# A graph and LSTM kernel whose row gathers each wait for an earlier gather to land

## The chip, the cores and the metric

The kernel runs on one core of one Trainium2 chip. The metric is the device time of one execution in microseconds (us), from the first to the last instruction and what the device adds around them. The engines are named as in the profile: PE (TensorE, matrix products), PEld (its weight loads), DVE (VectorE), ACT (ScalarE), POOL (GpSimd) and SP (SyncE, which only issues transfers here). A name with a q behind it (PEldq, SPq, POOLq) is that engine's sequencer, which handles waits, branches and register loads.

## The reference

Three stages are computed. The second one, the graph stage, is the one that the change touches.

```
n = layernorm(x)                                  # 6250 nodes x 512
agg = segment_sum(n[src], dst, 6250)              # 100000 edges, sorted by dst
h = relu((n + agg) @ W1 + b1)
x = x + relu(h @ W2 + b2)
# then, over 50 groups of 125 rows, as an LSTM:
f, i, o = sigmoid([z_t, h] @ W + b); g = tanh(...)  # z = layernorm(x)
c = f * c + i * g;  h = o * tanh(c)
x = x + hs
```

All of it is float32. `src` and `dst` are only known when the kernel runs, so rows of the normalized table are fetched by index.

## The kernel before

**Three parts.** `table_part` (0 to 189 us of the span) writes the normalized table, already multiplied by W1, to DRAM. `graph_part` (189 to about 1616 us) goes through 50 blocks of 125 destination nodes. `lstm_part` takes the rest. The change is in `graph_part` alone.

**One block of the graph stage.** The edges of a block are cut into 16 columns of 128 edges (`COLUMNS = 16`); the few edges beyond 2048 (7 blocks have some) are handled by a branch that is taken at run time. Each column goes through four engines:

- POOL issues an indirect DMA, the gather (line 811), which fetches 128 rows of 2 KB from `ln_table` into one of 16 buffers `rows` (in the profile `kept`, because they lie in the same memory as the LSTM's tensor of that name). It waits on `s_low` for DVE to be done with the buffer's last content, 16 gathers ago. When it has landed, it adds 16 to `s_rows[j]`, one semaphore for each of the 16 buffers.
- ACT (line 851) rounds the rows to a short format, `high` (in the profile `shared`). It waits for the landing on `s_rows[j]`, and on `s_visit` for PE to be done with what the same one of the 8 `high` buffers held.
- DVE (line 1014) subtracts to get `low_part` and adds 1 to `s_low`. It also makes the one-hot matrices (line 1006).
- PE (line 904) multiplies one-hot by high and by low into `agg`, and adds 1 to `s_visit`. One such pair is called a visit.

**The layers of the block before** run between the columns. DVE adds `agg` to the block's own table rows (`hin`, line 1053) when PE has raised `s_agg`, which it does with the first product behind the block's last visit; for block 0 a `drain` does it (line 989). PE turns `hin` (line 918), ACT applies relu (line 863), PE multiplies by W2 (lines 950, 954), DVE forms x1 and its statistics, ACT makes `z` and rounds the turned `z` (`zT_high`, line 886), and PE makes the four banks of gate inputs `gps` (line 924), which DVE adds to biases (line 1035) and SP stores.

**What sets the order.** Each engine's instructions stand in a fixed order in its function `one`, and every exchange is a semaphore. POOL's part is written out for all 50 blocks, 16 gathers one behind the other, with the branch for extra edges behind each block. The other engines run a loop over the blocks. `range_of` (line 727) loads three numbers of a block (edges before, extra columns, first edge) from `ranges` into registers with one TENSOR_LOAD; SP calls it for each load of edge lists, and ACT, PE and DVE call it once for each block. POOL calls it inside its branch only, and reads the number of extra columns of five blocks at once (line 738).

Of the kernel before, what the change touches and what calls it, by code (L numbers as in the profile page):

```python
# [42 lines left out]
LANDED = 16  # L43
# [554 lines left out]
def graph_part(nc, x, edges, table, x1_rows, gate_rows, Wx, W2s, b1c, b2r, bgr, s_w, WEIGHTS_LOADED,  # L598
# [24 lines left out]
    with ExitStack() as ctx:  # L623
        LATER = K // 2
        LAST = LATER + 1
        MOST = -(-E // P)
# [41 lines left out]
        s_rows = [sem(ctx, f"s_rows{j}") for j in range(LANDED)]  # L668
# [57 lines left out]

        def range_of(e, b):
            _, (before, extra, begin) = nc.values_load_multi_w_load_instructions(
                ranges[0:1, bass.ds(b, 1), 0:3].rearrange("o b n -> o (b n)"), engines=[e.engine],
                min_val=0, max_val=E, skip_runtime_bounds_check_because="the first part bounds it")  # L730
            extra = nc.s_assert_within(extra, 0, MOST, skip_runtime_bounds_check_because="the first part bounds it")
            begin = nc.s_assert_within(begin, 0, E, skip_runtime_bounds_check_because="the first part bounds it")
            return before, extra, begin

        CHECKED = 5

        def extras_of(e, b):
# [5 lines left out]
        def beyond_of(e, visit):  # L743
            def beyond(b):
                before, extra, begin = range_of(e, b)
                with e.If(extra > 0):
                    with e.Fori(0, extra) as g:
                        visit(before + g, g, begin)
            return beyond
# [4 lines left out]
        def _(e):  # L754
# [4 lines left out]
            def load_ends(b):  # L759
                begin = range_of(e, b)[2]  # L760
                if not isinstance(b, int) or b > 0:
                    hold(e, s_passed, s_ends, b * 16)
                e.dma_start(ends[:, bass.ds(b, 1), :, :].rearrange("p o n two -> p (o n two)"),
                            edges[bass.ds(begin, P * COLUMNS)].rearrange("(p n) two -> p (n two)", p=P)
                            ).then_inc(s_ends, 16)
# [40 lines left out]
        def _(e):  # L806
            def gather(n, b, j):
                if j == 0:
                    hold(e, s_passed, s_ends, b * 16 + 16)
                e.wait_ge(s_low, n + 1)  # L810
                e.indirect_dma_start(  # L811
                    out=rows[j % RING][:, :], out_offset=None, in_=table[:, :],
                    in_offset=bass.IndirectOffsetOnAxis(ap=ends[:, b, j, 0:1], axis=0),
                ).then_inc(s_rows[j % LANDED], 16)
# [16 lines left out]
            for b in range(BLOCKS):  # L831
                if b % CHECKED == 0:
                    extras = extras_of(e, b)
                for j in range(COLUMNS):
                    gather(b * COLUMNS + j, b, j)
                with e.If(extras[b % CHECKED] > 0):
                    before, extra, begin = range_of(e, b)
                    with e.Fori(0, extra) as g:
                        gather_beyond(before + g, g, begin)
# [7 lines left out]
        def _(e):  # L847
# [4 lines left out]

            def high_beyond(n, g, begin):
# [44 lines left out]
        def _(e):  # L898
# [8 lines left out]

            def visit_beyond(n, g, begin):
                e.wait_ge(s_hot_x, n + 2)
# [87 lines left out]
        def _(e):  # L997
# [18 lines left out]

            def beyond_columns(n, g, begin):
                e.wait_ge(s_visit_x, n + 1)
# [980 lines left out]
```

## Time and profile before

| what | value |
|---|---|
| time, median of 3 runs | 2981.14 us (2975.06 to 2987.83) |
| span of the profiled execution | 2970.5 us |
| PE busy over the span | 2593.4 us (87%) |
| DVE, ACT, POOL busy | 2147.9, 1564.9, 1009.0 us |
| gathers, line 811 | 800, mean 1046 ns of POOL each |
| queue of POOL's transfers (q0) | 240.39 MB |
| queue of SP's transfers (q1) | 370.08 MB |

The page gives no time for the profiled execution other than its span. A row that groups instructions is read so: line, engine, operation, output<-inputs, count, busy time, mean, and then the time for which the engine had been idle just before, with what ended that idle time. "remote" stands where the trace found no instruction that ended the wait. Busy PE time is partly modelled: the ends of matrix products are not measured.

### The profile page before, as it was taken

Reading aid. Unit: us, or ns where it says so; the run is one execution under the profiler, and the core shown is the slowest. Engines: PE = TensorE matmul, PEld = TensorE weight load, DVE = VectorE, ACT = ScalarE, POOL = GpSimd, SP = SyncE. Lnnn points to the kernel's source line nnn. Section 1 sums busy time; section 2 is a strip of 40 time slices with the busy share of each in tenths; the row PEclk is TensorE's granted clock in tenths of the full one; section 3 lists DMA queues with packets and bytes.
Section 4 is the critical chain, followed back from the end, with each engine's and each line's share of the span. In section 5 each row is a group of like instructions: output and inputs, shape, how many; then the busy total and the mean of one; then the engine's idle time right before and its main releaser. Section 6 shows DMA issues by size and latency. Waiting matters only on the chain. (4 is left out here: it accounts for less than half of the span.)

```text
span 2970.5 us, 47617 instructions
## 1 busy us (share of the span) xinstructions
PE 2593.4 (87%) x10746; PEld 1893.3 (64%) x10747; DVE 2147.9 (72%) x5785; ACT 1564.9 (53%) x3986; POOL 1009.0 (34%) x1018
## 2 busy tenths in 40 slices
PE   7966988878889888898888799899999799989997
PEld 6844766657667666676666566666666455655554
DVE  7745766767777677676676588777777777768886
ACT  5643444444444444444443566566656576757775
POOL 0236656655666566565653100000000000013333
PEclk9978999989999998899989899999999899999998
DMA  9657776767777777677766776577777666569995
GB/s 239 182 146 210 209 218 202 221 198 208 220 220 220 214 214 214 197 217 211 216 205 199 194 190 169 173 241 239 237 241 236 169 171 171 166 158 251 252 253 142
DMA packets 194202, 611.09 MB, mean 206 GB/s; under 512 B 41822, under 2 KB 47966, under 8 KB 164394
## 3 DMA queue, kind: packets, MB, share of 16 engines
q1 hardware_dynamic: 120432, 370.08, 42.0%
q0 software_dynamic: 73712, 240.39, 29.6%
q8 instruction: 18, 0.29, 0.0%
q14 instruction: 40, 0.33, 0.0%
HBM read 468.71 MB, written 141.62 MB: 205 GB/s over the span
## 5 line engine op out<-in xcount | busy, mean ns | idle before, releaser
L811 POOL DMA_INDIRECT kept<-ln_table,kept x800 | 836.7, 1046 | 554.7 <-DVE shared L1014 307.6
L1502 PE MATMUL acc<-shared,state 128*125 128x512 f32 x2244 | 775.0, 416 | 62.8 <-DVE state L1798 47.3
L851 ACT ACTIVATE shared<-kept 128x512 fp32r<-128x512 f32 x800 | 449.3, 626 | 403.7 <-remote 223.3
L1502 PEld LDWEIGHTS acc<-shared,state 128*125 128x125 f32 x2244 | 401.2, 187 | 198.9 <-ACT acc L1433 66.1
L904 PE MATMUL agg<-shared,onehot 128*125 128x512 f32 x1200 | 433.4, 463 | 33.0 <-DVE shared L1014 17.3
L1343 POOL TENSOR_TENSOR out<-h,lx 125x512 f32<-125x512 f32 x50 | 64.5, 1289 | 1122.6 <-DVE h L1823 1122.6
L904 PEld LDWEIGHTS agg<-shared,onehot 128*125 128x125 f32 x1200 | 254.1, 220 | 104.5 <-issue 37.1
L1502 PE MATMUL acc<-W_low,state 128*125 128x512 f32 x800 | 316.5, 396 | 0.0
L1502 PE MATMUL acc<-last_high,state 128*125 128x512 f32 x748 | 298.6, 399 | 0.0
L1014 DVE TENSOR_TENSOR shared<-kept,shared 128x512 fp32r<-128x512 f32 x400 | 267.1, 687 | 14.8 <-ACT shared L851 7.6
L924 PE MATMUL gps<-Wx_high,zT_high 128*125 128x512 f32 x800 | 226.0, 405 | 39.6 <-ACT zT_high L886 33.7
L1014 DVE TENSOR_TENSOR low_part<-kept,shared 128x512 fp32r<-128x512 f32 x400 | 256.2, 689 | 2.9 <-issue 2.5
L924 PE MATMUL gps<-Wx_low,zT_high 128*125 128x512 f32 x800 | 223.9, 402 | 0.0
L924 PE MATMUL gps<-Wx_high,zT_low 128*125 128x512 f32 x800 | 210.6, 395 | 0.0
L924 PEld LDWEIGHTS gps<-Wx_high,zT_high 128*125 128x125 f32 x800 | 152.1, 191 | 83.9 <-issue 44.7
L1425 ACT ACTIVATE tc<-c 125x128 f32<-125x128 f32 x600 | 153.7, 303 | 91.3 <-DVE c L1815 91.1
L1399 ACT ACTIVATE gate<-acc 125x512 f32<-125x512 f32 x200 | 119.6, 598 | 155.5 <-PE acc L1502 154.8
L1805 DVE TENSOR_TENSOR c<-gate,c 125x256 f32<-125x256 f32 x300 | 126.2, 421 | 84.5 <-ACT gate L1399 82.7
L924 PEld LDWEIGHTS gps<-Wx_low,zT_high 128*125 128x125 f32 x800 | 152.9, 191 | 38.7
L904 PE MATMUL agg<-low_part,onehot 128*125 128x512 f32 x400 | 165.5, 414 | 9.9 <-issue 9.7
L924 PEld LDWEIGHTS gps<-Wx_high,zT_low 128*125 128x125 f32 x800 | 148.5, 186 | 37.6
L1502 PEld LDWEIGHTS acc<-W_low,state 128*125 128x125 f32 x800 | 150.3, 188 | 30.8
(235 smaller groups left out, 4295.4 us busy)
## 6 DMA issues: line engine op xcount, KB each, us to landing
xg<-total_rows SPq DMA_DIRECT2D x100, 896.0 KB
xg<-gate_rows SPq DMA_DIRECT2D x88, 896.0 KB
gate_rows<-gout SPq DMA_DIRECT2D x200, 224.0 KB
total_rows<-total SPq DMA_DIRECT2D x50, 896.0 KB
kept<-ln_table,kept POOLq DMA_INDIRECT x800
lx<-x_rows POOLq DMA_DIRECT2D x50, 250.0 KB, 7.3
out_dram<-out POOLq DMA_DIRECT2D x50, 250.0 KB, 2.9
held<-in_x_dram SPq DMA_DIRECT2D x25, 448.0 KB
```

The lines of the kernel that those rows point to most:

```text
L811: e.indirect_dma_start(out=rows[j % RING][:, :], out_offset=None, in_=table[:, :], in_offset=bass.IndirectOffsetOnAxis(ap=ends[:, b, j, 0: ...
L851: e.activation(high[j % PARTS][:, :], rows[j % RING][:, :], ACT.Copy).then_inc(s_high, 1)
L904: m = e.matmul(agg[0:L, :], onehot[:, j % HOT_RING, :], part[j % PARTS][:, :], start=(j == 0 and part is high), stop=(part is low_part), s ...
L924: products.append(e.matmul(gps[n][0:L, :], state[:, k, :], weights[:, k, n // 2, n % 2].rearrange("p s c -> p (s c)"), start=(begins and k ...
L1014: e.tensor_tensor(low_part[j % PARTS][:, :], rows[j % RING][:, :], high[j % PARTS][:, :].bitcast(F32), ALU.subtract).then_inc(s_low, 1)
L1343: e.tensor_tensor(out[par][0:L, :], h[par][0:L].rearrange("c k u -> c (k u)"), x1[par][0:L, :], ALU.add).then_inc(s_out, 1)
L1399: e.activation(gates[0:L, half, 0].rearrange("c s u -> c (s u)"), sums, ACT.Sigmoid).then_inc(s_fi[half], 1)
L1425: e.activation(cell_turned[0:L, k], cell[0:L, k], ACT.Tanh).then_inc(s_tc[k], 1)
L1502: m = e.matmul(acc[n][0:L, :], stationary[:, k, :], weights[k][:, n * PAIR:(n + 1) * PAIR], start=begins, stop=(k == K - 1), skip_group_ch ...
L1805: e.tensor_tensor(half_of(cell, half), gates[0:L, half, 0, 0].rearrange("c (k u) -> c k u", k=KH), half_of(cell, half), ALU.mult).then_inc ...
```

## The change

Before gather n is issued, POOL also waits until gather n-3 has landed (`FLYING = 3`), on the same `s_rows` semaphores on which ACT waits. Beside it, `range_of` is taken apart in three functions of one number each, so that each place loads only what it uses; in the branch for extra columns that makes two loads where there was one.

```diff
-        def range_of(e, b):
-            _, (before, extra, begin) = nc.values_load_multi_w_load_instructions(
-                ranges[0:1, bass.ds(b, 1), 0:3]...
+        def extra_of(e, b):
+            _, (extra,) = nc.values_load_multi_w_load_instructions(
+                ranges[0:1, bass.ds(b, 1), 1:2]...
+        def begin_of(e, b):
+            _, (begin,) = ... ranges[0:1, bass.ds(b, 1), 2:3]...
+        def before_of(e, b):
+            _, (before,) = ... ranges[0:1, bass.ds(b, 1), 0:1]...
+                min_val=0, max_val=BLOCKS * MOST)
 
         CHECKED = 5
+        FLYING = 3
...
             def beyond(b):
-                before, extra, begin = range_of(e, b)
+                extra = extra_of(e, b)
                 with e.If(extra > 0):
+                    before = before_of(e, b)
                     with e.Fori(0, extra) as g:
-                        visit(before + g, g, begin)
+                        visit(before + g)
...
             def load_ends(b):
-                begin = range_of(e, b)[2]
+                begin = begin_of(e, b)
...
                 e.wait_ge(s_low, n + 1)
+                if n >= FLYING:
+                    e.wait_ge(s_rows[(n - FLYING) % LANDED], ((n - FLYING) // LANDED + 1) * 16)
                 e.indirect_dma_start(
...
                 with e.If(extras[b % CHECKED] > 0):
-                    before, extra, begin = range_of(e, b)
+                    extra, begin = extras[b % CHECKED], begin_of(e, b)
+                    before = before_of(e, b)
```

On POOL, at the start of the second block, a gather waited for the edge list and a free buffer, and the next 15 for a free buffer alone; behind them stand the branch and the extra gather (before):

```order
L811 DMA kept<-ln_table,kept 128x512 [waits s_ends_loaded,s_low]
L811 DMA kept<-ln_table,kept 128x512 [waits s_low] x15
L836 COMPARE_AND_BRANCH
L728 TENSOR_LOAD ranges
L838 UNCONDITIONAL_BRANCH
L838 ISA
```

The same place now:

```order
L825 DMA kept<-ln_table,kept 128x512 [waits s_ends_loaded,s_rows13,s_low]
L825 DMA kept<-ln_table,kept 128x512 [waits s_rows14,s_low]
L825 DMA kept<-ln_table,kept 128x512 [waits s_rows15,s_low]
L825 DMA kept<-ln_table,kept 128x512 [waits s_rows0,s_low]
L825 DMA kept<-ln_table,kept 128x512 [waits s_rows1,s_low]
```

No gather has moved; each has one more semaphore, that of the gather three before it, across the border between blocks too.

On DVE, behind the last column of the first block, with the branch for extra columns (before):

```order
L1014 TENSOR_TENSOR low_part<-kept,shared 128x512 x4
L728 TENSOR_LOAD ranges
L746 COMPARE_AND_BRANCH
L747 UNCONDITIONAL_BRANCH
L747 ISA
```

The same place now:

```order
L1029 TENSOR_TENSOR low_part<-kept,shared 128x512 x4
L728 TENSOR_LOAD ranges
L757 COMPARE_AND_BRANCH
L740 TENSOR_LOAD ranges
L740 ISA x2
L759 UNCONDITIONAL_BRANCH
L759 ISA
```

The load that every block makes has one number instead of three; the added load (line 740) stands inside the branch. ACT and PE have the same piece.

## Rows read from the trace of the kernel before

**Rows 1.** Busy time by engine (count), clock, DMA share, GB/s: the graph stage.

```profile
189.00:1616.00 1427.00, 1196.28 (x4880) 928.27 (x4881) 987.58 (x1935) 629.86 (x1296) 848.00 (x814) 0.90 0.71 211
```

**Rows 2.** Who waited for whom: us in total, times, longest.

```profile
DVE hin L1053 <- remote: 160.1, 40, 5.1
...
PE hin_turned L918 <- DVE hin L1053: 123.0, 35, 4.8
...
PE gps L924 <- ACT zT_high L886: 33.7, 7, 12.0
```

**Rows 3.** Timeline of POOL, one block: start, us, instruction, idle before and releaser.

```profile
817.32 1.46 POOL L811 DMA_INDIRECT kept<-ln_table,kept  x1 [2.30 <-DVE shared L1014]
...
830.78 0.95 POOL L811 DMA_INDIRECT kept<-ln_table,kept  x1 [0.30 <-issue]
835.77 1.16 POOL L811 DMA_INDIRECT kept<-ln_table,kept  x1 [4.05 <-DVE shared L1014]
```

**Rows 4.** Timeline of PE, the same block's end.

```profile
826.81 0.39 PE L904 MATMUL agg<-low_part,onehot 128*125 128x512 f32 x1
...
828.90 2.02 PE L924 MATMUL gps<-Wx_high,zT_low 128*125 128x512 f32 x8
834.38 0.65 PE L918 MATMUL hin_turned<-ident,hin 125*128 125x125 f32 x4 [3.46 <-DVE hin L1053]
```

**Rows 5.** Timeline of ACT, the same stretch.

```profile
833.59 0.63 ACT L851 ACTIVATE shared<-kept 128x512 fp32r<-128x512 f32 x1 [5.46 <-remote]
835.06 1.13 ACT L863 ACTIVATE between<-hin_turned,b1c 128x125 f32<-128x125 f32 x4 [0.84 <-PE hin_turned L918]
```

**Rows 6.** Timeline of DVE, the same stretch.

```profile
833.63 0.69 DVE L1053 TENSOR_TENSOR hin<-agg,hin 125x512 f32<-125x512 f32 x1 [4.63 <-remote]
...
834.82 0.68 DVE L1014 TENSOR_TENSOR shared<-kept,shared 128x512 fp32r<-128x512 f32 x1
```

**Rows 7.** The drain of line 989: ns least, median, most, and its start.

```profile
L989 PEldq DRAIN  x1: 21098/21098/21098, 215.2 to 215.2; - x1
```

**Rows 8.** Timeline of POOL and DVE at that drain's end, and the engines meanwhile.

```profile
232.81 0.95 POOL L811 DMA_INDIRECT kept<-ln_table,kept  x1 [0.30 <-issue]
...
236.34 0.69 DVE L1053 TENSOR_TENSOR hin<-agg,hin 125x512 f32<-125x512 f32 x1 [17.18 <-PEq L989]
...
216.00:234.00 18.00, 0.00 (x0) 0.00 (x0) 2.48 (x4) 3.15 (x5) 13.50 (x15) 0.50 0.74 210
```

**Rows 9.** A later long stop: engines in one stretch, POOL's last gather, ACT's next work.

```profile
592.00:600.00 8.00, 0.00 (x0) 0.00 (x0) 0.00 (x0) 0.00 (x0) 5.05 (x6) 0.78 0.71 213
...
597.62 0.95 POOL L811 DMA_INDIRECT kept<-ln_table,kept  x1 [0.30 <-issue]
...
601.53 0.59 ACT L886 ACTIVATE zT_high<-z_turned 128x500 fp32r<-128x500 f32 x1 [13.11 <-remote]
```

**Rows 10.** Timeline of POOL and ACT: the first two gathers and what they release.

```profile
189.30 0.99 POOL L811 DMA_INDIRECT kept<-ln_table,kept  x1 [32.59 <-DMA kept<-edges]
190.60 0.95 POOL L811 DMA_INDIRECT kept<-ln_table,kept  x1 [0.30 <-issue]
...
192.92 0.63 ACT L851 ACTIVATE shared<-kept 128x512 fp32r<-128x512 f32 x1 [10.89 <-DMA kept<-ln_table,kept]
195.42 0.63 ACT L851 ACTIVATE shared<-kept 128x512 fp32r<-128x512 f32 x1 [1.88 <-DMA kept<-ln_table,kept]
```

**Rows 11.** Timeline of POOL and DVE around a block with an extra column.

```profile
571.31 0.96 POOL L811 DMA_INDIRECT kept<-ln_table,kept  x1 [0.30 <-issue]
...
576.84 0.98 POOL L824 DMA_INDIRECT rows_x<-ln_table,slab_x  x1 [3.95 <-DMA slab_x<-edges]
...
550.41 0.69 DVE L1053 TENSOR_TENSOR hin<-agg,hin 125x512 f32<-125x512 f32 x1 [4.80 <-remote]
573.72 0.69 DVE L1053 TENSOR_TENSOR hin<-agg,hin 125x512 f32<-125x512 f32 x1 [0.46 <-remote]
```

**Rows 12.** Register loads of line 728 on DVE: ns least, median, most.

```profile
L728 DVEq TENSOR_LOAD <-ranges x50: 743/748/998, 213.0 to 1618.7; - x50
```

More of the change, by code:

```diff
@@ L725, in no_columns @@
             pass
-        def range_of(e, b):
-            _, (before, extra, begin) = nc.values_load_multi_w_load_instructions(
-                ranges[0:1, bass.ds(b, 1), 0:3].rearrange("o b n -> o (b n)"), engines=[e.engine],
-                min_val=0, max_val=E, skip_runtime_bounds_check_because="the first part bounds it")
-            extra = nc.s_assert_within(extra, 0, MOST, skip_runtime_bounds_check_because="the first part bounds it")
-            begin = nc.s_assert_within(begin, 0, E, skip_runtime_bounds_check_because="the first part bounds it")
-            return before, extra, begin
+        def extra_of(e, b):
+            _, (extra,) = nc.values_load_multi_w_load_instructions(
+                ranges[0:1, bass.ds(b, 1), 1:2].rearrange("o b n -> o (b n)"), engines=[e.engine],
+                min_val=0, max_val=MOST, skip_runtime_bounds_check_because="the first part bounds it")
+            return extra
+        def begin_of(e, b):
+            _, (begin,) = nc.values_load_multi_w_load_instructions(
+                ranges[0:1, bass.ds(b, 1), 2:3].rearrange("o b n -> o (b n)"), engines=[e.engine],
+                min_val=0, max_val=E, skip_runtime_bounds_check_because="the first part bounds it")
+            return begin
+        def before_of(e, b):
+            _, (before,) = nc.values_load_multi_w_load_instructions(
+                ranges[0:1, bass.ds(b, 1), 0:1].rearrange("o b n -> o (b n)"), engines=[e.engine],
+                min_val=0, max_val=BLOCKS * MOST)
+            return before
         CHECKED = 5
+        FLYING = 3
         def extras_of(e, b):
@@ L851, in high_part, with high_beyond @@
                 e.activation(high[j % PARTS][:, :], rows[j % RING][:, :], ACT.Copy).then_inc(s_high, 1)
-            def high_beyond(n, g, begin):
+            def high_beyond(n):
                 hold(e, s_passed, s_go_x, n + 1)
@@ L906, in visit, with visit_beyond @@
                 m.then_inc(s_visit, 1)
-            def visit_beyond(n, g, begin):
+            def visit_beyond(n):
                 e.wait_ge(s_hot_x, n + 2)
@@ L1015, in low_of_rows, with beyond_columns @@
                                 high[j % PARTS][:, :].bitcast(F32), ALU.subtract).then_inc(s_low, 1)
-            def beyond_columns(n, g, begin):
+            def beyond_columns(n):
                 e.wait_ge(s_visit_x, n + 1)
```

## The prediction

> **What bounds the kernel now.** I cut the span into its stages first. The graph stage takes 1427 us for 50 blocks, 28.5 us each; PE is busy for 1196 us of it, POOL for 848, and the transfers fill 71% of the 16 DMA engines [rows 1]. No engine is full, so the stage is set by waits, and the second view was who waits for whom. The largest on the way to PE has no known releaser: DVE before `hin`, 160.1 us in 40 blocks; PE sits idle for 123.0 us behind that DVE wait. Another, of PE for ACT's `zT_high`, is rarer (7 times, 33.7 us) but up to 12.0 us long [rows 2].
>
> Third, the timeline of one block, engine by engine, to find what "remote" is. PE's last visit is recorded to end at 827.20 (826.81 + 0.39), and the first product behind it, which raises `s_agg`, starts at once. Yet ACT, which needs that visit, and DVE, which needs `s_agg`, start at 833.59 and 833.63 [rows 4 to 6]. Their other inputs are old: ACT's rows come from a gather about 19 us earlier, DVE's table rows from a load about 25 us earlier. When both are let go, PE turns `hin` at 834.38 and ACT has the result at 835.06, 0.03 us after the turning is recorded to end. So at that moment PE's semaphores arrive promptly, while 6.4 us before they did not. The clearest case is the drain: it starts at 215.2, takes 21.1 us and ends with DVE's start at 236.34, though PE has nothing to compute from 216 to 234 [rows 7, 8]. From 592 to 600 us PE, DVE and ACT all do nothing, ACT waiting for a turning that was recorded long before [rows 9].
>
> What do these have in common? POOL is issuing gathers without a pause: 11 of them from 817.32 to 830.78 in the typical block [rows 3], and a longer chain in the two others. The release follows POOL's last gather start by 2.8 us (830.78 to 833.59), by 3.5 us (232.81 to 236.34) and by 3.9 us (597.62 to 601.53) [rows 3, 5, 8, 9]. One more case is a natural experiment: in a block with an extra column POOL stops behind the gather of 571.31 until 576.84; DVE's wait there is 0.46 us instead of 4.80, and `hin` follows the previous one after 23.31 us [rows 11]. I read this as: while a dense stream of gathers runs, something lets PE's completion signals through only slowly; it needs a pause in the stream. The trace does not show what.
>
> **The change, part by part.** *The added wait.* 797 gathers get one more condition. What is its size? The first gather starts at 189.30 and ACT sees it at 192.92, 3.6 us; the second, with SP's loads beside it, takes from 190.60 to 195.42, 4.8 us [rows 10]. POOL restarts 0.27 us after the signal that it waits for (DVE ends at 835.50, POOL starts at 835.77) [rows 3, 6]. Three gathers can therefore start every 3.9 to 5.1 us, one per 1.30 to 1.70 us. Now the plain distance is 1.25 us (0.95 + 0.30), and 1.35 us on average over the 11 of rows 3, where some take 1.4 us of POOL. With landings of 3.6 us the wait hardly binds: about 0.05 us on the dense half of the chain, 0.3 us for a block. With landings of 4.8 us it adds 0.35 us to each, 3.6 us for the ten distances. I take a third of the gathers at the slow landing, because SP's stores and loads fill about a third of the block's time: 1.3 us for each chain. Behind the waiting gather stand only POOL's later gathers, and each is needed by ACT some 18 us later (issue at about 814, use at 833.59), so this delay alone is covered. POOL has the room too: 16 gathers at 1.30 to 1.70 us are 21 to 27 us, against 28.5 us for a block [rows 1]. The cover is gone if landings average above 5.1 us.
>
> *What the wait may remove.* It acts when landings grow late, the time when the stream is densest relative to what the transfers do. Lower bound of the effect: nothing, because at most a few hundredths of a microsecond are added between gathers. Upper bound: all of the unexplained stop. In PE's idle time this is 123.0 us behind `hin`, 21.1 us at the drain and 33.7 us behind the `zT_high` waits [rows 2, 7]: 178 us. On top comes the clock: in this stage the granted share is 0.90 [rows 1], since PE comes out of each idle stretch at the lower level of 1.2 GHz instead of 2.4; with no stops some 5% of 1196 us, 60 us, could return. The nearest row to full success is the 23.31 us block of rows 11, made with a real pause of 5.5 us, while the change makes pauses of tenths. So I take half: PE's stops -90 us, clock -30 us. Against that the chain ends 1.3 us later where a stop remains, some 20 blocks, +15 us after rounding down for overlap. Sum about -105 us.
>
> *The taken-apart register load.* The load costs 0.75 us now [rows 12] for three numbers, on four engines' sequencers; with one number it can cost between nothing and 0.75 us, so at most 50 x 0.75 = 37 us would be saved if it were on the path. It stands where DVE and PE have work queued and where ACT runs into the long stop a few columns later, so I take 0. Where the stops vanish ACT could gain a few tenths per block; I leave that in the range. In the 7 extra blocks there is one more load, at most 0.75 us each, 5 us.
>
> Against the profiled span of 2970.5 us the sum gives 2865; the median of the runs stands 10.6 us above that span, so the time is about 2875 us.
>
> One rule of the Trainium skill speaks against this reading. Its page "Perfetto Trace Analysis", in the section on TensorE's instructions, says that the profiler computes the end of a matrix product and does not observe it. By that rule PE's visits could really be late and the missing time would be PE at work, which no cap on gathers gives back: the sum would be 0. The rows speak against it on one point, the products between the visit and the turning, as told in the first rival.
>
> **The rivals.** *First: PE is really busy, or the wait never binds.* If PE were behind, it would have finished the visit only at 833.59, and then 15 products recorded 0.23 us apart (3.5 us) would have to run before the turning; but ACT holds the turned result at 835.06 [rows 4, 5], 1.5 us later. So real lateness of PE is unlikely, but that three in flight is simply what the stream has already (3.6 us of landing at 1.25 us distance is 2.9 gathers) is quite possible. Then nothing changes: 2981 us, within 10.
>
> *Second: the stop stays, and the chain is longer.* This is the slower side. In the present loop `hin` is released about 2.8 us behind POOL's 11th gather, and POOL's chain starts a fixed path behind `hin`. If a stream at 1.35 to 1.7 us is still too dense, each microsecond added to the chain is added to the block: 1.3 us x 41 blocks (those with a wait) = +53 us, 3034 us; with slow landings throughout 3.6 x 41 = +148 us. It decides from the point where the stop ends with POOL's chain, as now, and landings exceed about 3.8 us. For it: the streams of rows 8 and 9 move 210 GB/s at only 0.71 to 0.74 of the DMA engines, so it isn't a full DMA that holds PE's signals, and three in flight may be as bad as before. Against it: if the landing signals are held back as PE's are, POOL pauses by itself and ends the stop.
>
> *Third: the stop goes altogether.* Then a block takes the larger of 23.3 us [rows 11] and POOL's 16 x 1.43 = 23 us plus its waits, say 24.5 us: 50 x 4 = -200 us, 2781 us.
>
> **How the numbers follow.** The forecast, half of the stop removed, has 0.33; the third rival 0.15; nothing changes 0.22; the slower one 0.30. A measurement of this kernel tells about 0.5% (15 us) from no change. Faster by more is 0.48 (forecast and third rival), within 0.22, slower by more 0.30. The likeliest is 2875 us, its own range 2820 to 2950. To hold 8 in 10 the range goes from 2770 into the slower case up to 3045; the long-landing end of that case and the best end of the third rival are left out. Both signs are in it, and I can't make it narrower honestly, since the trace has no run with the stream thinned a little.
>
> **What the profile after would show.** Right: POOL's gathers wait for a landing (a new releaser, the rows' DMA) with distances of 1.3 to 1.7 us; DVE's wait before `hin` falls from 4.6 us to about 2 and its total from 160 to about 80 us; the clock of the stage rises above 0.90; the drain at block 0 falls well below 21 us. Wrong in the direction of the first rival: POOL's distances stay at 1.25 and 1.35 us. Wrong in the direction of the second: the distances grow, the waits before `hin` stay at or above 4.6 us, and the block takes over 28 us with its release still 2 to 4 us behind POOL's last gather. Landings above 5.1 us on average would make POOL the bound, with ACT waiting for rows.

## The result and the profile after

The changed kernel takes 2990.12 us (median of 11 runs, 2984.78 to 2996.56), the kernel before 2975.06 us in as many runs on the same chip (2965.07 to 2987.83). The ratio is 1.0042, 95% interval [1.0028, 1.0056]: 0.4% slower, which is the same within 2%, where 2875 us, 3.6% faster, was forecast. (One later run of the kernel before, at a granted clock of 0.65, took 3532 us and is in no ratio here.)

The stage view first, columns as in [rows 1]. The graph stage has grown from 1427 to 1441 us. PE is idle for 1441.00 - 1210.37 = 231 us of it, as before (1427.00 - 1196.28 = 231 us), and the granted clock has hardly moved, 0.91 for 0.90. So the change has not given PE anything back; the question is what it waits for now.

```profile
189.00:1630.00 1441.00, 1210.37 (x4879) 927.08 (x4880) 996.33 (x1926) 667.48 (x1293) 842.85 (x814) 0.91 0.71 208
```

The view of who waited for whom, changed kernel, columns as in [rows 2] (L866 is ACT's rounding, L883 its `h1T_high`, L965 PE's first layer-2 products, L825 the gather, L1068 `hin`):

```profile
ACT shared L866 <- DMA kept<-ln_table,kept: 643.1, 516, 10.5
...
PE late L965 <- ACT h1T_high L883: 166.2, 43, 5.6
POOL kept L825 <- DMA kept<-ln_table,kept: 180.1, 147, 3.0
...
PE hin_turned L933 <- DVE hin L1068: 18.8, 9, 5.7
...
DVE hin L1068 <- remote: 2.9, 7, 0.6
```

The unexplained stop of [rows 2] is gone, not halved: DVE's wait before `hin` fell from 160.1 us in 40 blocks to 2.9 us in 7, PE's behind it from 123.0 to 18.8 us. In its place stands a wait that hardly existed: ACT now waits 643.1 us, 516 times, for the rows themselves (20.8 us in 13 before), and PE 166.2 us for ACT's `h1T_high`. The same view of ACT in the kernel before:

```profile
ACT shared L851 <- remote: 223.3, 49, 7.2
...
ACT shared L851 <- DMA kept<-ln_table,kept: 20.8, 13, 10.9
```

The drain of [rows 7] and the registers of [rows 12] answer too:

```profile
L1004 PEldq DRAIN  x1: 309/309/309, 218.3 to 218.3; - x1
```

```profile
L728 DVEq TENSOR_LOAD <-ranges x50: 299/304/550, 216.6 to 1633.8; - x50
```

The drain takes 0.309 us, not 21.1. A register load of one word takes 0.304 us on DVE's sequencer (median) where that of three took 0.748.

How a late row becomes a late PE is seen in one block of the changed kernel (timelines of POOL, ACT, DVE and PE; the instruction's start, its length, and in brackets the idle time before it with what ended it):

```profile
803.01 0.95 POOL L825 DMA_INDIRECT kept<-ln_table,kept  x1 [1.43 <-DMA kept<-ln_table,kept]
805.63 0.94 POOL L825 DMA_INDIRECT kept<-ln_table,kept  x1 [1.68 <-DMA kept<-ln_table,kept]
...
804.95 0.63 ACT L866 ACTIVATE shared<-kept 128x512 fp32r<-128x512 f32 x1 [1.99 <-DMA kept<-ln_table,kept]
...
809.29 0.63 ACT L866 ACTIVATE shared<-kept 128x512 fp32r<-128x512 f32 x1 [1.91 <-DMA kept<-ln_table,kept]
810.90 0.63 ACT L866 ACTIVATE shared<-kept 128x512 fp32r<-128x512 f32 x1 [0.98 <-DMA kept<-ln_table,kept]
811.43 1.11 ACT L878 ACTIVATE between<-hin_turned,b1c 128x125 f32<-128x125 f32 x4
812.42 0.72 ACT L883 ACTIVATE h1T_high<-between 128x250 fp32r<-128x250 f32 x2
...
803.66 0.68 DVE L1068 TENSOR_TENSOR hin<-agg,hin 125x512 f32<-125x512 f32 x1
...
804.39 0.65 PE L933 MATMUL hin_turned<-ident,hin 125*128 125x125 f32 x4 [0.47 <-DVE hin L1068]
...
812.90 0.79 PE L965 MATMUL late<-W_high,h1T_high 128*125 128x512 f32 x1 [4.84 <-ACT h1T_high L883]
```

`hin` starts at 803.66 without a wait and PE turns it at 804.39; that signal is prompt now. ACT could apply relu at about 805, but its instructions stand in a fixed order and four roundings stand between 804.95 and L878; the rows of the last two come at 809.29 and 810.90. So PE waits 4.84 us at L965, where the stop of [rows 4] cost it 3.46 us. And POOL's restart is seen in the first two lines and the third: ACT takes the row landed at 804.95, POOL starts its next gather at 805.63, 0.68 us later.

The first gathers [rows 10] show the same: starts 1.29 and 1.26 us apart, then the fourth one waits for the first to land.

```profile
188.29 0.99 POOL L825 DMA_INDIRECT kept<-ln_table,kept  x1 [32.12 <-DMA kept<-edges]
189.58 0.95 POOL L825 DMA_INDIRECT kept<-ln_table,kept  x1 [0.30 <-issue]
190.84 0.95 POOL L825 DMA_INDIRECT kept<-ln_table,kept  x1 [0.30 <-issue]
192.00 0.63 ACT L866 ACTIVATE shared<-kept 128x512 fp32r<-128x512 f32 x1 [10.52 <-DMA kept<-ln_table,kept]
...
192.71 1.46 POOL L825 DMA_INDIRECT kept<-ln_table,kept  x1 [0.93 <-DMA kept<-ln_table,kept]
```

Pairing each of the 800 gathers with ACT's use of it: where ACT was waiting (539 gathers), the landing takes 4.05 us in the median, 4.38 us on average, one in ten over 5.67 us. POOL starts again 0.68 us after ACT does (380 cases, most of them within 0.01 us). Three in flight thus give one gather per (4.38 + 0.68)/3 = 1.69 us, 27.0 us for 16. Measured over the stage, the distance inside a block is 1.68 us on average; the rest of the 28.8 us stands at the border between blocks, where the first gather starts 3.63 us behind the one before it (2.8 us on average in 42 blocks, 8.4 us in the 7 behind an extra column).

```profile
818.89 1.02 POOL L825 DMA_INDIRECT kept<-ln_table,kept  x1 [0.70 <-issue]
821.06 0.64 ACT L866 ACTIVATE shared<-kept 128x512 fp32r<-128x512 f32 x1 [2.22 <-DMA kept<-ln_table,kept]
821.74 1.28 POOL L825 DMA_INDIRECT kept<-ln_table,kept  x1 [1.83 <-DVE shared L1029]
```

This is a border (POOL, ACT, POOL), and it shows a trap in the view: POOL's wait is put down to DVE, which frees the buffers, and the view of who waited has 105.1 us of such waits in 76 cases. But no gather of the changed kernel waited for a buffer: DVE had released each one at least 14.0 us before the gather started (from DVE's end to POOL's start, all 784 from the second block on). POOL starts 0.68 us behind ACT's start on a landed row here too, so the wait is for the landing. Before the change a row was asked for 18.5 us ahead of its use (median), now 4.3 us ahead.

### The profile page after: what moved, and what is told of

Its sections match the earlier page's. It is cut to its first block and busy times, and to the rows that moved or that the text cites. A ratio compares the mean times of both kernels' runs of the same rounds, so it can differ in the third digit from the quotient of the medians.

```text
span 2983.2 us, 48519 instructions
## 1 busy us (share of the span) xinstructions
PE 2606.0 (87%) x10746; PEld 1889.9 (63%) x10747; DVE 2160.6 (72%) x5785; ACT 1604.8 (54%) x3986; POOL 1004.5 (34%) x1018
## 5 line engine op out<-in xcount | busy, mean ns | idle before, releaser
L825 POOL DMA_INDIRECT kept<-ln_table,kept x800 | 831.2, 1039 | 593.9 <-issue 244.1
L866 ACT ACTIVATE shared<-kept 128x512 fp32r<-128x512 f32 x800 | 497.2, 630 | 684.2 <-DMA kept<-ln_table,kept 643.1
L919 PE MATMUL agg<-shared,onehot 128*125 128x512 f32 x1200 | 391.3, 419 | 24.9 <-DVE shared L1029 16.7
L919 PEld LDWEIGHTS agg<-shared,onehot 128*125 128x125 f32 x1200 | 223.0, 194 | 98.1 <-issue 21.8
L965 PE MATMUL late<-W_high,h1T_high 128*125 128x512 f32 x200 | 118.2, 591 | 180.3 <-ACT h1T_high L883 167.8
L965 PEld LDWEIGHTS late<-W_high,h1T_high 128*125 128x125 f32 x200 | 54.7, 274 | 214.7 <-ACT h1T_high L883 187.3
L1073 DVE TENSOR_TENSOR h1T_low<-between,h1T_high 128x500 fp32r<-128x500 f32 x50 | 34.1, 682 | 204.1 <-ACT h1T_high L883 200.8
```

The source lines that it names most:

```text
L825: e.indirect_dma_start(out=rows[j % RING][:, :], out_offset=None, in_=table[:, :], in_offset=bass.IndirectOffsetOnAxis(ap=ends[:, b, j, 0: ...
L866: e.activation(high[j % PARTS][:, :], rows[j % RING][:, :], ACT.Copy).then_inc(s_high, 1)
L919: m = e.matmul(agg[0:L, :], onehot[:, j % HOT_RING, :], part[j % PARTS][:, :], start=(j == 0 and part is high), stop=(part is low_part), s ...
L965: e.matmul(late[0:L, :], h1T.high[:, k, :], weights[:, k, :], start=(k == 0 and weights is W2s.high), stop=False, skip_group_check=True)
```

## The experiments

**Theory A:** the stop is removed whole, and the chain of gathers takes its place as the bound. **Rivals:** B, the late signals are only moved elsewhere; and, once they could be compared, P (the pace of POOL's gathers makes PE's signals late) against Q (the number in flight does). C, in the earlier expectations, is what later became P: dense issue on POOL, in some sessions, whatever the number in flight. In the expectations for fly4 and fly6, A and B stand for what is written there.

A surprise must be told first. The kernel before took one of two times, the same throughout one session of runs: about 2695 us in four sessions, and 2956 or 2983 us in two, as in the result. The traces of its kin show the difference: in the first kind no wait is put down to "remote", in the second there are about 100. I call the sessions prompt and late. Four of the five chips of the experiments were seen in one kind each; one was late and, some 8 minutes later, prompt. Every ratio below is to the kernel before in the same session.

| kernel | session | us | ratio to before [95%] | us per block | median distance of gathers | "remote" waits, us (times) |
|---|---|---|---|---|---|---|
| before | late (the result) | 2975.1 | 1 | 28.3 | 1.25 | 466.5 (97) |
| changed | late (the result) | 2990.1 | 1.0042 [1.0028, 1.0056] | 28.8 | 1.58 | 6.1 (8) |
| split_only | prompt | 2693.9 | 0.9995 [0.9986, 1.0005] | 22.9 | 1.25 | 0 |
| split_only_again | late | 2952.4 | 0.999 [0.9964, 1.0017] | 27.8 | 1.25 | 443.4 (102) |
| fly2 | prompt | 3411.5 | 1.2661 [1.2634, 1.2688] | 37.3 | 2.24 | 0 |
| fly3_again | prompt | 2982.5 | 1.1058 [1.1038, 1.1079] | 28.9 | 1.58 | 0 |
| fly4, fly4_again, fly4_third | prompt | 2815.5, 2817.3, 2819.2 | 1.0446, 1.0454, 1.0464 | 25.6 | 1.27 | 0 |
| fly4_fourth | late | 2919.8 | 0.9803 [0.9751, 0.9854] | 27.6 | 1.33 | 451.2 (110) |
| fly6, fly6_again | prompt | 2691.6, 2692.5 | 0.9984 [0.9973, 0.9996], 0.9976 [0.9966, 0.9986] | 23.0 | 1.25 | 0 |
| fly6_third | late | 2951.6 | 0.9985 [0.9951, 1.002] | 28.0 | 1.26 | 505.9 (103) |
| pause12, pause12_again | prompt | 2865.2, 2865.5 | 1.0626, 1.064 | 26.5 | 1.25 | 0 |
| half_uncapped | late | 2936.0 | 0.9919 [0.9893, 0.9945] | 27.8 | 1.22 | 458.4 (98) |
| half3 | late | 2886.5 | 0.9783 [0.9725, 0.9841] | 26.8 | 1.31 | 358.2 (106) |
| thin | prompt | 2964.3 | 1.1002 [1.0955, 1.1049] | 28.4 | 1.54 | 0 |
| thin_again | late | 2970.7 | 0.9968 [0.995, 0.9985] | 28.4 | 1.54 | 0 |
| thin1 | prompt | 2772.7 | 1.0295 [1.0191, 1.0399] | 24.4 | 1.31 | 0 |

(Blocks: first to last start of `hin`, over 49. Distances: POOL's starts from 300 to 1200 us. Remote waits: from 189 to 1500 us. fly2, fly4_third, fly4_fourth, thin, thin1 and pause12_again are medians of two runs, the others of at least four. The intervals of fly4_fourth and half3 contain 0.98: both are faster, and whether by 2% is open.)

**split_only and split_only_again: the register loads alone.** The functions `extra_of`, `begin_of` and `before_of` as in the change, without

```diff
-                if n >= FLYING:
-                    e.wait_ge(s_rows[(n - FLYING) % LANDED], ((n - FLYING) // LANDED + 1) * 16)
```

> The changed kernel without the added wait: only the register load taken apart (0.75 us to 0.30 us in each block on ACT, DVE and PE). Theory: the load stands beside other work, so the time is that of the kernel before, within 8 us, DVE's unexplained wait before hin stays near 160 us in all. Rival: the load is on the path of each block, then 50 x 0.45 us = 22 us less than before, and the added wait alone cost some 35 us.

> The register loads split, no wait. Ratio 1.00 to the kernel before on any chip: 2695 us where that takes 2695, 2975 where it takes 2975. On a chip of the second kind its trace would show the wait before hin that the two chips so far do not show.

Both ratios are 1.00: loading one word instead of three buys nothing in time, as the prediction took it. The larger use of this kernel is as a stand-in for the one before in both kinds of session. The stage view (columns as in [rows 1]), split_only in the prompt session, its whole graph stage and the steady part:

```profile
189.00:1333.00 1144.00, 1107.71 (x4883) 876.07 (x4884) 986.83 (x1934) 640.43 (x1296) 858.51 (x813) 0.99 0.86 262
500.00:1200.00 700.00, 689.97 (x3080) 550.43 (x3079) 613.12 (x1206) 395.61 (x804) 532.34 (x500) 1.00 0.87 264
```

and the same steady stretch in the late session (split_only_again):

```profile
500.00:1200.00 700.00, 603.05 (x2505) 471.53 (x2504) 498.02 (x979) 314.80 (x653) 419.31 (x405) 0.92 0.73 215
```

With prompt signals PE is busy for 690 of 700 us at the full granted clock: the same matrix products, 4883 of them, fill a stage of 1144 us, 22.9 us per block. That settles the prediction's first rival: the missing 283 us of the stage (1427 - 1144) were no work. They are 194 us of PE's idle time (231 us fell to 36) and 89 us of its busy time (1196.28 to 1107.71 us for the same products, at a granted clock of 0.99 for 0.90). The Trainium skill says on its page "Perfetto Trace Analysis", section "Tensor Engine Instruction (MATMUL, LD_WEIGHTS)", that a product's end is computed; read against the stop that was a warning, but the time comes back with the same products, so here the rule hid nothing. POOL's gathers stood no less dense in that session; the trace below has them 1.25 and 1.38 us apart, without a pause at all. So a dense stream does not by itself delay a signal.

```profile
703.73 0.95 POOL L823 DMA_INDIRECT kept<-ln_table,kept  x1 [0.30 <-DVE shared L1027]
704.98 0.94 POOL L823 DMA_INDIRECT kept<-ln_table,kept  x1 [0.30 <-issue]
706.23 1.08 POOL L823 DMA_INDIRECT kept<-ln_table,kept  x1 [0.31 <-DVE shared L1027]
707.61 0.95 POOL L823 DMA_INDIRECT kept<-ln_table,kept  x1 [0.30 <-issue]
```

In the late session the waits of [rows 2] are back (split_only_again, who waited for whom):

```profile
ACT shared L864 <- remote: 219.5, 50, 7.4
DVE hin L1066 <- remote: 156.3, 40, 6.6
...
PE hin_turned L931 <- DVE hin L1066: 127.7, 37, 8.4
```

The semaphore updates that the traces record say the same more directly. In the block of [rows 3] to [rows 6] the product that raises `s_agg` is recorded to end at 827.44, the update comes at 833.61 and `hin` starts at 833.63. From the product's end to the update it takes 6.13 us in the median of 48 blocks of the kernel before, and 0.01 us in each of 49 blocks of split_only. So it is the signal that is late, and DVE starts 0.02 us behind it.

The late sessions have one more mark, which no view prints: a part of the semaphore updates is missing from their traces, of DVE's and ACT's and of the landings too. split_only has 49,050 updates on record, split_only_again, the same code, 32,620. The 800 gathers raise `s_rows` 16 times each, 12,800 in all; 12,808 updates of these semaphores are recorded in the first and 4,533 in the second. The changed kernel has 38,741 in the late session of the result and 49,050 in a prompt one (fly3_again), though it hardly waits for late signals in either (6.1 and 0 us). So this mark tells the kind of a session from a trace without remote waits, and it leaves a rival for the cause of the late signals that nothing here tests: that they come with the recording of the updates itself. Every trace here records them.

**fly2, fly4, fly6: other caps.** `FLYING = 3` becomes 2, 4 or 6; nothing else.

> FLYING = 2: gather n waits for the landing of gather n-2. Theory (in the changed kernel the gathers themselves are the bound: a landing seen after 4.05 us at the median and 4.4 on average, and POOL starting again 0.68 us behind it): two gathers per 4.7 to 5.1 us, 2.45 us each, 39 us for the 16 of a block against 28.8, 50 x 10 us = +500 us, near 3490 us. Rival (POOL has slack, the time is set elsewhere): below 3100 us.

> FLYING = 4. The landing chain allows one gather per (4.4 + 0.68) / 4 = 1.27 us, hardly more than the 1.25 us that POOL takes anyway, so gathers are no longer the bound. Theory A (a cap near the natural number in flight still breaks the dense stream where landings grow late): the unexplained wait before hin stays small, a block takes about 25 us, near 2850 us. Theory B (only a stream thinned to three in flight lets PE's signals through): the wait before hin is back at 4.6 us a block and the time is that of before, 2975 us within 10.

> FLYING = 6: binds only where a landing takes over 7 us. Theory A: near 2900 us, since the longest pile-ups are still cut. Theory B: as before, 2975 us within 8, the wait before hin near 160 us in all.

In prompt sessions the mean landings where ACT waits are 3.93, 4.36 and 4.57 us with 2, 3 and 4 in flight; with 0.68 us for the restart the chain's step comes to 2.31, 1.68 and 1.31 us. Measured medians: 2.24, 1.58 and 1.27 us; at 4 POOL's own 1.25 us is nearly reached, yet the mean is 1.58 us (1.43 us in split_only) and the block 25.6 us. I read this as each landing above the mean stopping POOL, with nothing to make up for it. At 6 the wait seldom binds and the time is that without a cap, 0.2% under it in two sessions. The expectations for fly4 and fly6 took the kernel before at 2975 us; here it took 2694.5 us, so 2815.5 and 2691.6 us miss all of their figures and do not decide between the theories. fly2's 3411.5 us lies 80 us below the 3490 us expected, far from its rival.

**fly3_again, fly4_again, fly6_again: the changed kernel itself, beside the other caps.** Unchanged code of the change, of fly4 and of fly6.

> The changed kernel itself, beside the kernel before on whichever chip this is. Theory A (the change replaced one bound by another: a gather chain of (4.38 us mean landing + 0.68 us restart) / 3 = 1.69 us, so 27 to 29 us per block of 16): about 2980 to 3000 us on every chip. Where the kernel before takes 2975 us here, the ratio is 1.004; where it takes 2695 us as on the chip of the first four experiments, the ratio is about 1.11. Rival B (the changed kernel's time is set by the same late completion signals as before, only elsewhere): on a chip where the kernel before takes 2695 us it would take about 2700 us, ratio 1.00.

> FLYING = 4. Theory A: chain (4.38 + 0.68) / 4 = 1.27 us, about 20 to 22 us per block plus the stretches in which it is late: 2815 us as on the other chip, whatever the kernel before takes here (ratio 0.946 where that is 2975, 1.045 where it is 2695). Rival B: where the kernel before takes 2975 us, 4 gathers in flight do not remove the late signals, and the time is 2975 or more.

> FLYING = 6. Theory A with the stop tied to how many gathers are under way: where the kernel before takes 2975 us here, a cap of 6 trims only the bursts and gives between 2700 (the stop goes) and 2975 us (it stays); I expect 2800. Where the kernel before takes 2695 us, ratio 0.998. Rival C (the late signals are a matter of the chip and of dense issue on POOL, not of the number under way): 2975 us, ratio 1.00.

The session was prompt again, and the changed kernel took 2982.5 us, 0.3% from its 2990.1 us in the late one, while the kernel before went from 2975 to 2697 us. Theory A holds and B falls: the changed kernel has its own bound and does not see the kind of session. The view of who waited (fly3_again, 189 to 1500 us) is that of the changed kernel, whose first line in the same stretch is 583.2 us in 469 cases:

```profile
ACT shared L866 <- DMA kept<-ln_table,kept: 587.1, 469, 10.9
POOL kept L825 <- DMA kept<-ln_table,kept: 191.2, 167, 3.0
DVE h1T_low L1073 <- ACT h1T_high L883: 180.0, 44, 6.0
```

So 1.004 is the ratio of two unrelated times that lie close together, 28.3 us per block for the late signals and 28.8 us for the chain. Priced alone, in a prompt session, the cap costs 10.6%.

**pause12 and pause12_again: one pause in each block.** In the changed kernel the wait is replaced:

```diff
-                if n >= FLYING:
-                    e.wait_ge(s_rows[(n - FLYING) % LANDED], ((n - FLYING) // LANDED + 1) * 16)
+                if j in (12,):
+                    e.wait_ge(s_rows[(n - 1) % LANDED], ((n - 1) // LANDED + 1) * 16)
```

> No cap; instead gather 12 of each block waits for the landing of gather 11, so that POOL stops once per block, about when the signals are needed for hin. Theory A with a stop caused by an unbroken run of gathers: where the kernel before takes 2975 us, the wait before hin falls and the time is 2750 to 2850 us; where it takes 2695 us, a pause of about 4.4 + 0.7 us per block is covered by the lead of 18 us or costs at most 50 x 2 us: 2695 to 2800. Rival C: 2975 us where before takes 2975.

> One pause of POOL per block (gather 12 waits for the landing of gather 11), the others as dense as before. Where the kernel before takes 2960 to 2980 us: if the late signals come with an unbroken run of dense gathers, they go in part, 2870 to 2950 us; if they depend on the mean pace alone (1.74 us in the kernel before, which a stop slows by itself), they stay, 2975 us or more. Where it takes 2695 us: 2865 us as measured before.

Both sessions were prompt: 2865 us twice, 3.6 us more per block for a pause of a landing and a restart. That is far above the 2800 us allowed for, because with prompt signals there is no lead of 18 us to cover it: in split_only rows are issued 6.2 us ahead of their use (median). What a pause does to late signals remains untested.

**half3 and half_uncapped: half the bytes.** From the second block on only 64 of 128 rows are fetched, so the products of the other half work on old rows and that part of the computation is left out, with the cap of 3 (half3) and on split_only (half_uncapped):

```diff
-                    out=rows[j % RING][:, :], out_offset=None, in_=table[:, :],
-                    in_offset=bass.IndirectOffsetOnAxis(ap=ends[:, b, j, 0:1], axis=0),
+                    out=rows[j % RING][0:P if b == 0 else P // 2, :], out_offset=None, in_=table[:, :],
+                    in_offset=bass.IndirectOffsetOnAxis(ap=ends[0:P if b == 0 else P // 2, b, j, 0:1], axis=0),
```

> The changed kernel (FLYING = 3) whose gathers, from the second block on, fetch only 64 of the 128 rows (the other half of each tile keeps old rows, so this part of the computation is left out). It tells whether the chain's step (4.36 us mean landing + 0.68 us restart, over 3) is a fixed latency or the time of the bytes. Theory A1 (mostly latency): the landing falls by less than 1 us, to about 3.6 us, the chain's step is (3.6 + 0.68)/3 = 1.43 us, 23 to 25 us per block, and the time about 2790 to 2850 us, still bound by the chain. Theory A2 (mostly bytes): the landing halves to about 2.2 us, the step would be 0.96 us and not bind, and the time is that without a cap, about 2695 us or less. I expect A1, 2820 us.

> The control of half3: the same half gathers without the wait. If POOL's own time per gather (1.04 us + 0.27 us between two, 21 us of a 23 us block) is what holds the kernel at 2695 us where the stop is absent, this gets shorter only as far as the half gather costs POOL less; if PE's own work is the bound there, the time stays within 1% of 2695 us. I expect 2650 to 2695 us. Where the kernel before takes 2975 us: rival C (late signals come with the dense issue on POOL) says 2950 or more, a stop tied to the bytes of the gathers says under 2850.

The session was late. A gather ends in 16 packets of four bytes on its queue, one for each raise of `s_rows`, and the end of the last of them times every landing, waited for or not. Measured so, from POOL's start and from the second block on, a whole gather lands after 3.61 us in the median and 3.89 us on average (changed kernel, late session), a half one after 2.70 and 2.86 us (half3); without a cap it is 3.98 us on average for whole ones (split_only_again) and 2.80 us for half ones (half_uncapped). Half the bytes take 1.0 to 1.2 us off: three quarters of a landing stay, nearer to A1 than to A2. By that, an estimate, the bytes of a whole gather make about 2 of its 3.9 us. The total of 2886.5 us lies above A1's range, since late signals are in it. The Trainium skill's page "DMA: Bandwidth & Descriptors", section "Anatomy of one DMA — SWDGE (gpsimd) path", has a fixed cost of about 2 us and the rest by bytes; by its fit, an estimate, 256 KB would take 2.6 us and half of it 2.3. The traces do not agree: beside this kernel's other traffic the level is 3.9 us, and the half costs 1.0 us less, not 0.3.

That is the other finding: with gathers 1.31 us apart the late signals came back (half3, who waited for whom), where 1.58 us had removed them. Without the cap, a third less traffic in the steady part (141 for 215 GB/s) left them nearly whole: 136.5 us before `hin` for 156.3, and 458.4 us in all for 443.4. So bytes are not what holds the signals. half_uncapped took 2936.0 us, between the 2950 us of C and the 2850 us of a stop tied to bytes, and its waits decide for C.

```profile
ACT shared L866 <- remote: 162.8, 54, 9.9
...
DVE hin L1068 <- remote: 76.3, 30, 7.2
```

**fly6_third and fly4_third.** Code of fly6 and fly4.

> FLYING = 6 once more. Where the kernel before takes 2695 us: ratio 0.998. Where it takes 2975 us: 2700 us if the late signals come with more than 6 gathers under way, 2975 us if they do not depend on it.

> FLYING = 4. Its step is 1.31 us, that of POOL itself. Where the kernel before takes 2960 us: theory P says that the late signals stay, at least in part (2880 to 2960 us, ratio 0.97 to 1.00); theory Q says that they go (2815 us, ratio 0.95). Where it takes 2695 us: 2815 us, ratio 1.045 as twice before.

A cap of 6 leaves the late signals as they are (159.4 us before `hin` in 39 blocks). fly4_third fell on a prompt session and repeats fly4.

**thin and thin_again: the pace without the wait.** On split_only, behind each gather:

```diff
+                for m in (2 * n, 2 * n + 1):
+                    e.wait_ge(s_pace, m)
+                    e.memset(pace[:, :], 0.0).then_inc(s_pace, 1)
```

> The register loads split, no wait for landings; instead two small memsets (128x96, about 0.18 us each and a wait for each) stand behind every gather on POOL, so that a gather starts every 1.7 to 1.9 us, as with FLYING = 3, whatever has landed. Theory P (where the kernel before takes 2960 us, it is the pace of the gathers on POOL that makes PE's signals late): the waits named remote before hin go away as with FLYING = 3, and the time is set by the pace, 50 x 16 x 1.8 us plus what lies around, 2880 to 3000 us. Theory Q (it is the wait for landings, that is the few gathers in flight, that removes them): the remote waits stay with the slower pace, 3000 us or more. Where the kernel before takes 2695 us there are no such waits, and the pace alone gives 2850 to 2980 us by either.

> The slower pace without a wait for landings, once more. Where the kernel before takes 2960 us, theory P says 2965 us (what it took on the other kind of chip) without remote waits before hin; theory Q says that those stay, 3000 us or more. Where it takes 2695 us: 2964 us.

**fly4_fourth.** Code of fly4, in the same session as thin_again.

> FLYING = 4 once more, for a chip on which the kernel before takes about 2960 us. There theory P (the pace of the gathers on POOL makes PE's signals late) says that they stay, at least in part: 2880 to 2960 us, ratio 0.97 to 1.00. Theory Q (few gathers in flight remove them) says 2815 us, ratio 0.95. Where the kernel before takes 2695 us: 2815 us, ratio 1.045.

thin_again had the late session: before at 2982.8 us, thin_again at 2970.7 us, without one remote wait. POOL's timeline (thin_again) shows what it does, 1.54 us from gather to gather at the least, and no wait for a landing:

```profile
700.16 0.95 POOL L826 DMA_INDIRECT kept<-ln_table,kept  x1 [0.16 <-issue]
701.11 0.43 POOL L832 MEMSET pace<- 128x96 f32 x2
701.70 1.12 POOL L826 DMA_INDIRECT kept<-ln_table,kept  x1 [0.15 <-issue]
702.82 0.43 POOL L832 MEMSET pace<- 128x96 f32 x2
703.40 0.95 POOL L826 DMA_INDIRECT kept<-ln_table,kept  x1 [0.16 <-DVE shared L1033]
```

Its largest waits are the changed kernel's, though nothing waits for a landing on POOL:

```profile
ACT shared L870 <- DMA kept<-ln_table,kept: 566.1, 453, 11.1
...
DVE h1T_low L1077 <- ACT h1T_high L887: 169.7, 42, 5.7
```

In the same session fly4 at 1.33 us kept its remote waits (fly4_fourth), 451.2 us in all as without a cap (443.4 in split_only_again) but less of them before `hin` (98.3 for 156.3), and took 2919.8 us:

```profile
ACT shared L866 <- remote: 216.6, 55, 13.2
DVE hin L1068 <- remote: 98.3, 29, 5.2
```

That thin_again's session was late shows in its own trace as well: 43,206 semaphore updates on record for 50,622 in thin.

A slower pace on POOL alone removes the late signals; the wait for landings is only one way to it. By itself this does not part P from Q, since a slower pace also leaves fewer gathers in flight. Counted by the last four-byte packets, at the start of a gather 1.71 earlier ones are under way on average in thin_again and 1.74 in the changed kernel, for 1.97 in the kernel before. half_uncapped parts them: its half gathers land sooner, only 1.24 are under way, and its late signals stay, at 1.22 us from gather to gather. In split_only, prompt, 2.60 are under way without a late signal. Q falls by these numbers, and by fly4_fourth, which it had at 2815 us; theory P stands. Pace here is that of the gathers with all that comes with each, 16 semaphore raises among it; which of these matters is not shown.

**thin1: a pace between.** thin with one memset behind each gather.

> thin with one memset behind each gather instead of two: about 0.22 us less between gathers, the smallest distance 1.32 us instead of 1.54 us (without a memset 1.25 us), the mean about 1.6 us instead of 1.77 us. Where the kernel before takes 2960 to 2980 us, theory P says that the late signals come back in part, as with FLYING = 4 (2920 us): 2850 to 2960 us; if there is a pace that removes them and costs less than that of thin, it shows here as 2850 us or less. Where it takes 2695 us: half of the cost of thin, about 2830 us.

Prompt session: 2772.7 us, below the expected 2830 us, since the mean distance came to 1.52 us and not 1.6. Whether 1.31 us is slow enough in a late session was not measured; half3 and fly4_fourth, at 1.31 and 1.33 us, kept 358.2 and 451.2 us of remote waits and speak against it.

## Why the prediction was wrong

The reading of the stop was right, as far as it went: completion signals that reach ACT and DVE late, bound to POOL's stream of gathers (though only in some sessions), with no work of PE behind them. It was shown by the recorded updates, by removing it in two ways (changed kernel, thin_again) and by a session without it. Point by point:

1. *Size of the added wait.* The prediction had landings of 3.6 to 4.8 us and one gather per 1.30 to 1.70 us; measured were 4.38 us on average and 1.69 us. That the rate lies at the end of the range is luck: that end paired a landing of 4.8 us with a restart of 0.27 us. A third of the gathers at the slow landing was too few, since 4.38 us lies two thirds of the way from 3.6 to 4.8; and **POOL's restart was taken as 0.27 us**, from a wait for DVE [rows 3, 6], where behind a landing it is 0.68 us.
2. *The cover.* This is the step that failed: "16 gathers ... are 21 to 27 us, against 28.5 us for a block" and "each is needed by ACT some 18 us later". Both 28.5 and 18 us were made by the stop itself. A block without it needs 22.9 us (the natural experiment of [rows 11] had already shown 23.31), and the gathers then run 6.2 us ahead, not 18. Measured against 22.9 us, the chain was the bound from the first: 16 x 1.69 = 27.0 us, 28.8 with the borders between blocks. The term "+1.3 us for each chain" measures 28.8 - 22.9 = 5.9 us per block, 50 x 5.9 = 295 us; fly3_again against before gives 285 us.
3. *What it removes.* Taken as half, -105 us with the chain's cost; it was all of it: with prompt signals the kernel is 281 us shorter (2975.1 to 2693.9 us, across sessions). The upper bound of 178 + 60 us was also too low: against split_only PE's idle time falls by 194 us and its busy time by 89 us, so the term of the clock was taken a third too small, and 16 us of idle time stood outside the rows read.
4. *The sum.* -281 + 295 = +14 us by these sizes, +15 us measured. Both terms come from the same three kernels' times, so this is a tally and no second proof; the independent one is that fly3_again took 2982.5 us in a prompt session, as the chain alone says. A gain and a loss of a tenth of the time each, where the prediction had -120 and +15.
5. *Register loads.* Taken as 0; 0.9995 and 0.999 say the same.

Of the rivals, the first (nothing changes, 2981 us within 10) has the measured 2990 us in its range by luck: it had a wait that never binds, and the distances grew from 1.25 to 1.58 us. The forecast's wide range, 2770 to 3045 us, holds the time too, and that says little. Of its signs, two came true, the drain and DVE's wait before `hin` (both further than forecast), and neither tells what the cap costs. The third (the stop goes altogether, 2781 us) had the removal right and the cost wrong in the same way: "24.5 us" per block took 1.43 us per gather. The second (slower) had the sign but not the mechanism: the stop did not stay. The prediction's warning of POOL as the bound, with ACT waiting for rows, is what happened, at landings of 4.4 us and not of 5.1, because the room was that of the block with the stop in it.

Open: what delays the signals, whether the recording of semaphore updates has a part in it, why only in some sessions, and whether a pace between 1.33 and 1.54 us would remove them at less cost. In prompt sessions fly6 is 0.2% faster than the kernel before; in the late one it is not told from it (0.9985, to 1.002). In a late session fly4 is 2.0% faster (two runs), and costs 4.5% in the others. No cap measured is a clear gain in both.

## What to carry to other kernels

Slack read from a kernel that is being stopped is slack made by the stop: before a wait is added "under cover", compare its chain with the block as it will be once the stop is gone. A cap on transfers in flight sets a rate, (landing + restart) / cap, and late landings count against it in full; price it by the mean landing and the measured restart behind a transfer. The releaser that a view names is the semaphore raised last, not always the one waited for: check it against the time at which each condition was met. And two times that agree within half a per cent need not have the same cause: run the suspect kernel where one of the causes is absent.

## What the runs showed of the hardware

- The same kernel took 2695 us or 2956 to 2983 us by session, with waits of ACT and DVE for PE's signals of up to 5.1 us before `hin`, 7.2 us before a rounding and 14.3 us before `zT_high` (kernel before), while POOL issued a gather per 1.25 us; one chip showed both kinds. At 1.33 us between gathers they were still there (fly4_fourth), at 1.54 us gone (thin_again). The traces of the late sessions lack part of the semaphore updates, a third of them without a cap (32,620 on record for 49,050, split_only_again and split_only).
- A gather of 128 rows of 2 KB landed 3.61 us after POOL's start, one of 64 rows 2.70 us (medians of the changed kernel and half3, to the last four-byte packet), and POOL was busy 0.94 and 0.90 us for them at the least. More in flight made it longer: 3.41, 3.88 and 4.11 us on average with caps of 2, 3 and 4, and 4.31 us without one (fly2, fly3_again, fly4, split_only).
- POOL went on 0.68 us after ACT had started on the same landing (median, changed kernel and fly2).
- A register load cost 0.30 us for one word and 0.75 us for three on DVE's sequencer, about 0.2 us for each further word. The Trainium skill's page "Runtime: NRT & Kernel Launch", section "Instruction fetch mechanics", has about 200 ns per register; the trace agrees for each further word, 0.22 us, and has 0.30 us for the first.
